# Graph blocks on one core: host-made transposes, norms applied on ScalarE, and a new step order

## The reference, cut to what matters

```python
# block 0
deg = jnp.sum(adj, axis=-1, keepdims=True)
agg = jnp.einsum('bij,bjf->bif', adj, x) / jnp.maximum(deg, EPS)
out = relu(einsum('bnf,of->bno', concatenate([x, agg], axis=2), W))
# block 1: three layers, relu after the first two
adj @ (x @ W) + b
# block 2: 8 heads of 64
attn = softmax(q k^T * scale, masked) * LA + LG * adj + LD * exp(-adj)
out = (attn @ v) @ W_out + b_out
# block 3
w = softmax(sum((q k^T * inv_scale) * adj, axis=-1), axis=nodes)
out = w * v
# after each block
(x - mean) / sqrt(var + 1e-5)
```

## Time and profile before

| | |
|---|---|
| median of 3 runs | 1419.85 us |
| the profiled execution | 1420.36 us |
| its span, first to last instruction | 1418.3 us |
| TensorE busy, share, matmuls | 1373.4 us, 97%, 11152 |
| VectorE busy, share | 1232.1 us, 87% |
| ScalarE busy, share | 921.4 us, 65% |
| GpSimd busy, share | 131.3 us, 9% |
| HBM read, written | 21.90 MB, 8.39 MB |
| mean granted clock of TensorE | 0.987 of 2.4 GHz |

### The profile page before, as it was taken

One profiled execution on the slowest core, in us unless ns is written; L12 is line 12 of the kernel. 1 busy time (PEld: TensorE's weight loads), 2 busy tenths in 40 slices (PEclk: granted clock), 3 DMA queues, 4 the chain that ended last, 5 costly groups with the idle time before them and its releaser, 6 DMA issues.

```text
span 1418.3 us, 30311 instructions
## 1 busy us (share of the span) xinstructions
PE 1373.4 (97%) x11152; PEld 1218.3 (86%) x11152; DVE 1232.1 (87%) x3821; ACT 921.4 (65%) x2445; POOL 131.3 (9%) x265
## 2 busy tenths in 40 slices
PE   4799999999999999999999999999999999999995
PEld 4788889888889888889888889888888888889884
DVE  4688889889889889889889889889889989889985
ACT  4466766666776666776666776666676666676662
POOL 0000001101001101001101001100001100001100
PEclk8899999999999999999999999999999999999997
DMA  4000000000000000000000000000000000000000
GB/s 146 17 17 17 24 24 2 24 24 25 24 24 4 22 24 25 24 25 9 17 24 24 24 25 11 15 25 24 24 25 20 6 25 24 24 25 9 1 9 22
DMA packets 34050, 32.22 MB, mean 23 GB/s; under 512 B 6896, under 2 KB 33392, under 8 KB 33904
## 3 DMA queue, kind: packets, MB, share of 16 engines
q1 hardware_dynamic: 33904, 30.30, 6.8%
HBM read 21.90 MB, written 8.39 MB: 21 GB/s over the span
## 4 chain that ended last, share of the span: by engine, by line
PE 96%; DVE 1%; ACT 1%; DMA 1%; issue 0%; POOL 0%; SPq 0%; POOLq 0%; DVEq 0%; ACTq 0%
PE psum L911 62%; PE psum L925 14%; PE psum L1143 9%; PE psum L1118 8%; PE psum L1192 1%; PE psum L1195 1%; DMA w_raw<-in_L_gnn_W 1%; PE psum L1205 0%; PE psum L1213 0%; DVE bn L561 0%; ACT wqkv_h L309 0%; POOL rstd L294 0%; DVE x L598 0%; ACT work L444 0%; DVE w_l L545 0%
## 5 line engine op out<-in xcount | busy, mean ns | idle before, releaser
L444 ACT ACTIVATE work<-work,shift 128x256 f32<-128x256 f32 x512 | 254.1, 500 | 16.5 <-DVE shift L738 16.5
L757 DVE SCALAR_TENSOR_TENSOR work<-work,rsum,extra 128x256 f32<-128x256 f32 x512 | 223.2, 478 | 1.4 <-DVE rsum L749 0.2
L738 DVE CUSTOM_DVE_ANT_0 work<-psum,minus_big 128x256 f32<-128x256 f32 x512 | 190.1, 419 | 2.2 <-PE psum L1118 1.6
L309 ACT ACTIVATE work<-psum 128x512 f32<-128x512 f32 x256 | 147.3, 591 | 10.0 <-PE psum L925 9.8
L291 POOL TENSOR_TENSOR mv<-mv,eps 128x2 f32<-128x2 f32 x128 | 34.4, 269 | 1272.8 <-DVE mv L582 1272.8
L911 PE MATMUL psum<-x2T_h,wqkv_h 128*128 128x256 f32 x512 | 149.2, 291 | 1.2 <-DVE x2T_l L545 1.2
L911 PE MATMUL psum<-x2T_l,wqkv_h 128*128 128x256 f32 x512 | 143.3, 280 | 0.0
L911 PE MATMUL psum<-x2T_h,wqkv_l 128*128 128x256 f32 x512 | 143.0, 279 | 0.0
L925 PE MATMUL psum<-ident,work 128*128 128x128 f32 x1024 | 139.8, 274 | 0.1
L1143 PE MATMUL psum<-work,v_sb 128*64 128x256 f32 x1024 | 131.9, 389 | 0.9 <-ACT work L309 0.7
L309 ACT ACTIVATE qkT_h<-psum 128x512 fp32r<-128x512 f32 x128 | 76.6, 599 | 85.7 <-PE psum L911 85.7
(11 more groups left out here) (138 smaller groups left out, 3858.1 us busy)
## 6 DMA issues: line engine op xcount, KB each, us to landing
x_sb<-in_x SPq DMA_DIRECT2D x32, 256.0 KB, 2.8
adj_sb<-in_adj SPq DMA_DIRECT2D x32, 256.0 KB, 3.0
out<-y_sb SPq DMA_DIRECT2D x32, 256.0 KB, 2.1
work<-in_L_gnn_W_qkv SPq DMA_DIRECT2D x1, 1536.0 KB, 9.0
mask_row<-in_nodemask SPq DMA_DIRECT2D x32, 32.0 KB, 3.4
w_raw<-in_L_gnn_W SPq DMA_DIRECT2D x3, 256.0 KB, 6.9
w_raw<-in_L_gnn_W SPq DMA_DIRECT2D x1, 512.0 KB, 8.2
wout_raw<-in_L_gnn_W_out SPq DMA_DIRECT2D x1, 512.0 KB, 9.8
```

The lines of the kernel that those rows point to most:

```text
L309: return nc.scalar.activation(dst, src, ACT.Copy, scale=scale)
L444: last = nc.scalar.activation(prob[:, p % 2, i, h], prob[:, p % 2, i, h], ACT.Exp, bias=shift[:, p % 2, h, i:i + 1], scale=-1.0, accum_out ...
L738: last = V_.tensor_tensor_reduce(out=prob[:, p % 2, i, h], in0=bank(SCORES[p] + h)[:, i * N:(i + 1) * N], in1=minus_big[:, g % 2, i], scal ...
L757: last = V_.scalar_tensor_tensor(out=prob[:, p % 2, i, h], in0=prob[:, p % 2, i, h], scalar=rsum[:, p % 2, h, i:i + 1], in1=extra[:, g % 2 ...
```

## The change

**Inputs.** The host hands in four more arrays: x and adj with their last two axes exchanged (`xT`, `adjT`), the weights of block 0 transposed in halves (`L0_gnn_WT`), and the two weights of block 3 joined and transposed (`L3_gnn_WT`); the three original weights of these blocks are no longer inputs. x and adj themselves are still loaded. `x_transpose`, `adj_transpose` and `weight_transposes` are gone from TensorE; the high and low parts are now made from SBUF instead of PSUM.

**Semaphores.** `dma_graph` is replaced by five pairs (`dma_x`, `dma_adj`, `dma_mask_row`, `dma_xT`, `dma_adjT`), and each step waits for its own input. At the start the transposed x and the weights of block 0 are issued first; the weights of block 3 come last and are split after those of block 2's output.

**Norms.** `norm_apply` moves from VectorE to ScalarE, as one ACTIVATE (Identity) per half with a scale and a bias per partition. GpSimd makes the bias, -mean x root, with two more operations per norm.

**Order and banks.** All four slot lists and the table of banks are new. Cut to its core:

```diff
-        XT = 6
-        ADJT = 2
-        SUP0 = 1
-        SELF = 7
-        AGG = 2
+        SUP0 = 7
+        SELF = 2
+        AGG = 6
...
+            def load_x(g):
+                fetch(xT_sb, xT_d, g, dma_xT)
+
+            def load_rest(g):
+                fetch(adjT_sb, adjT_d, g, dma_adjT)
+                fetch(adj_sb, adj_d, g, dma_adj)
+                fetch(x_sb, x_d, g, dma_x)
...
                 nc.gpsimd.tensor_tensor(mv[:, k, :, 1], mv[:, k, :, 1], eps[:, :], ALU.add) \
                     .then_inc(pool_var[k], 1)
+                nc.gpsimd.tensor_tensor(minus_mean[:, k], mv[:, k, :, 0], minus_one[:, :], ALU.mult) \
+                    .then_inc(pool_mean[k], 1)
                 pool.wait_ge(pool_var[k], once(g))
                 nc.gpsimd.tensor_tensor(rstd[:, k], mv[:, k, :, 1], minus_half[:, :], ALU.pow) \
+                    .then_inc(pool_pow[k], 1)
+                pool.wait_ge(pool_pow[k], once(g))
+                pool.wait_ge(pool_mean[k], once(g))
+                nc.gpsimd.tensor_tensor(minus_mean[:, k], minus_mean[:, k], rstd[:, k], ALU.mult) \
                     .then_inc(pool_rstd[k], 1)
...
-                act.wait_ge(pe_xT, once(g))
-                copy(fT[0][:, :, :], halves(bank(XT))).then_inc(act_xT, 1)
+                act.wait_ge(dma_xT[g % 2], loaded(g))
+                copy(fT[0][:, :, :], xT_sb[:, g % 2]).then_inc(act_xT, 1)
...
+            def norm_apply(k, g):
...
+                act.wait_ge(pool_rstd[k], once(g))
...
+                if k == 2:
+                    reuse(act, dve_x4_pre, once(g - 1))
...
+                for t in range(NT):
+                    last = nc.scalar.activation(dst[:, t], src[:, t], ACT.Identity, bias=minus_mean[:, k, t:t + 1],
+                                                scale=rstd[:, k, t:t + 1])
+                last.then_inc(act_y if k == 3 else act_x[k], 1)
...
-                pe.wait_ge(dve_x[0], once(g))
-                reuse(pe, act_probT, nth2(g - 1, 0, 1))
+                pe.wait_ge(act_x[0], once(g))
                 transpose_tiles(bank(X1T), x1).then_inc(pe_x1T, 1)
```

TensorE's new list, in which graph s - 1 is in block 1, s - 2 in attention and s - 3 in the tail:

```diff
             def slot(s):
+                qk(s - 2, 1)
+                tail_project(s - 3, HI)
+                tail_project(s - 3, LO)
+                scores(s - 2, 0)
+                scores(s - 2, 1)
+                tail_adj_k(s - 3)
+                values(s - 2, HI)
+                aggregate(s - 1, HI)
+                aggregate(s - 1, LO)
+                qk(s - 2, 2)
+                values(s - 2, LO)
+                qk(s - 2, 3)
+                probs_t(s - 2, 0, 0)
+                scores(s - 2, 2)
+                x1_transpose(s - 1)
+                probs_t(s - 2, 0, 1)
+                probs_t(s - 2, 1, 0)
+                support(0, s - 1, HI)
+                support(0, s - 1, LO)
+                probs_t(s - 2, 1, 1)
+                scores(s - 2, 3)
+                hidden(0, s - 1, HI)
+                hidden(0, s - 1, LO)
+                attend(s - 2, 0)
+                attend(s - 2, 1)
+                support(1, s - 1, HI)
+                support(1, s - 1, LO)
+                gate_row(s - 3)
+                probs_t(s - 2, 2, 0)
+                probs_t(s - 2, 2, 1)
+                hidden(1, s - 1, HI)
+                hidden(1, s - 1, LO)
+                probs_t(s - 2, 3, 0)
+                probs_t(s - 2, 3, 1)
+                attend(s - 2, 2)
+                support(2, s - 1, HI)
+                support(2, s - 1, LO)
+                attend(s - 2, 3)
+                gcn_out(s - 1, HI)
+                gcn_out(s - 1, LO)
+                support0(s, HI)
+                project_out(s - 2, HI)
+                project_out(s - 2, LO)
+                support0(s, LO)
+                x2_transpose(s - 1)
+                gate_column(s - 3)
+                self_product(s)
+                qk(s - 1, 0)
+                x3_transpose(s - 2)
```

More of the change, by code:

```diff
@@ new lines, in slot @@
+                exps(s - 6, 3, 1)
+                sup_hi(1, s - 5)
+                out_hi(s - 6, 0)
+                probs_t(s - 6, 2, 0)
+                probs_t(s - 6, 2, 1)
+                out_hi(s - 6, 1)
+                hidden(1, s - 5)
+                hidden_hi(1, s - 5)
+                probs_t(s - 6, 3, 0)
+                probs_t(s - 6, 3, 1)
+                sup_hi(2, s - 5)
+                x_hi(s - 4)
+                out_hi(s - 6, 2)
+                mask_bias(s - 4)
+                out_hi(s - 6, 3)
@@ new lines, in slot @@
+                gate_exps(s - 7)
+                adj_exp(s - 4)
+                norm_apply(1, s - 5)
+                x2_hi(s - 5)
+                gate_column(s - 7)
+                degrees(s - 4)
+                norm_apply(2, s - 6)
+                qk_hi(s - 5, 0)
+                sup0_hi(s - 4)
+                x3_hi(s - 6)
+                qk_hi(s - 5, 1)
+                tail_qkv(s - 6)
+                adj_hi(s - 4)
+                self_copy(s - 4)
+                norm_apply(3, s - 7)
@@ new lines, in slot @@
+                exps(s - 5, 0, 0)
+                exps(s - 5, 0, 1)
+                exps(s - 5, 1, 0)
+                qk_hi(s - 5, 2)
+                exps(s - 5, 1, 1)
+                values(s - 5)
+                norm_apply(0, s - 4)
+                qk_hi(s - 5, 3)
+                probs_t(s - 5, 0, 0)
+                x1_hi(s - 4)
+                probs_t(s - 5, 0, 1)
+                probs_t(s - 5, 1, 0)
+                sup_hi(0, s - 4)
+                probs_t(s - 5, 1, 1)
+                exps(s - 5, 2, 0)
@@ L533, in _ @@
+                exps(s - 5, 2, 1)
+                hidden(0, s - 4)
+                hidden_hi(0, s - 4)
             masks()
@@ new lines, in slot @@
+                scores(s - 4, 0, 0)
+                scores(s - 4, 0, 1)
+                adj_lo(s - 3)
+                scores(s - 4, 1, 0)
+                scores(s - 4, 1, 1)
+                tail_gate(s - 5)
+                aggregate(s - 3)
+                relu_residual(s - 3)
+                recip_sums(s - 4, 0)
+                norm_stats(0, s - 3)
+                norm_mean(0, s - 3)
+                probs(s - 4, 0, 0)
+                qk_lo(s - 4, 2)
+                recip_sums(s - 4, 1)
@@ new lines, in slot @@
+                probs(s - 4, 0, 1)
+                probs(s - 4, 1, 0)
+                probs(s - 4, 1, 1)
+                x1_lo(s - 3)
+                qk_lo(s - 4, 3)
+                scores(s - 4, 2, 0)
+                scores(s - 4, 2, 1)
+                sup_lo(0, s - 3)
+                scores(s - 4, 3, 0)
+                scores(s - 4, 3, 1)
+                recip_sums(s - 4, 2)
+                probs(s - 4, 2, 0)
+                probs(s - 4, 2, 1)
+                hidden_lo(0, s - 3)
@@ new lines, in slot @@
+                recip_sums(s - 4, 3)
+                probs(s - 4, 3, 0)
+                sup_lo(1, s - 3)
+                probs(s - 4, 3, 1)
+                out_lo(s - 4, 0)
+                gate_maximum(s - 5)
+                x1_bias(s - 3)
+                hidden_lo(1, s - 3)
+                adj_sum(s - 3)
+                sup_lo(2, s - 3)
+                out_lo(s - 4, 1)
+                x_lo(s - 2)
+                out_lo(s - 4, 2)
+                out_lo(s - 4, 3)
+                gcn_out(s - 3)
```

413 lines of the change are left out of this document (130 added, 283 removed).

## The result

| | before | after |
|---|---|---|
| median of 4 runs each | 1421.38 us | 1473.8 us |
| lowest, highest | 1418.3, 1423.34 | 1470.3, 1476.66 |
| the profiled execution, its span | 1420.36, 1418.3 | 1476.49, 1474.7 |

The changed kernel is slower: ratio 1.037, 95% interval 1.0333 to 1.0406. The prediction was 1412, and its range ended at 1437.

What follows compares the result with a forecast made beforehand. TensorE, without idle time at 42.36 us a slot, bounds the kernel. Savings of 1.24 less waits of 1.08 give 42.18; 1420.4 - 5.6 (31 slots) - 2.2 (ends) = 1412.6, said as 1412, range 1379 to 1437.

Steps and rivals of the forecast that it cites:

- The floor of TensorE in the new order: TensorE's starts per slot: 42.36 less 0.89 for transposes and 0.35 for fewer switches, 41.1 us.
- ScalarE's application: Norm application on ScalarE: 0.59 us one, pair ending at 1.08, against VectorE's pair at 0.74; +0.34.
- x3's wait: TensorE's wait at x3's transposes, from the end of project_out: 0.2 to 0.5, taken as 0.4 us.
- Three waits, 1.08 us a slot: TensorE waits before the x1, x2 and x3 transposes, summing to 1.08 us against 1.24 saved.
- GpSimd's part: Each norm, GpSimd's first start to the application: 1.00 us plus 0.37 for two added operations, about 1.37.
- x2: x2's transposes, from the end of gcn_out: cover 4.28 us against a chain of 4.69, wait 0.41.
- x1: x1's transposes, from the end of aggregate: cover 5.17 us against a chain of 5.44, wait 0.27.
- the parts outside the 31 slots: First and last graph: start -4.0, four lone norms +2.8, transposes and switches gone -1.0; sum -2.2 us.
- the bounds (0.27 to 0.8): Range for GpSimd's two added operations per norm, around 0.37 us.
- Rival 2: Norm chain outweighs savings at the three transposes through GpSimd's slow rows: slot 43.4, about 1450 us; chance 0.25.
- 0.89 us of transposes: TensorE, per graph: four adj transposes removed, 0.36 us, and four of x, 0.53 us.
- rival 3: VectorE's work sets the slot, so TensorE's saving is not given back: 42.36 stays, 1418 us; chance 0.06.

Runs made afterwards that it cites:

- quiet: Changed kernel with two VectorE steps, adj_extra and x2_bias, moved ahead of gcn_out and nothing removed; 1455.0 us.
- swap: Changed kernel with the two waits of VectorE's aggregate step back in the old order, TensorE's product first; 1462.42 us.
- one_pool: Changed kernel with the epsilon add and the mean's negation moved from GpSimd to VectorE, norms still applied on ScalarE; 1434.68 us.
- inputs_only: Kernel before with the host's transposed inputs alone, order and norms as before; 1411.77 us.
- norm_dve: Changed kernel with norms applied on VectorE again and two GpSimd operations a norm, transposed inputs and new order kept; 1448.55 us.
- quiet_dve: norm_dve with adj_extra and x2_bias ahead of gcn_out, aggregate's waits in the old order, and norm 1's application behind gate_probs; 1425.71 us.
- act_norm: Kernel before with norms applied on ScalarE and four GpSimd operations a norm, inputs and TensorE and VectorE order as before; 1502.28 us.
- ports: Separate kernel timing GpSimd's small operations alone and beside each kind of VectorE operation; root 0.67 us alone, 1.20 beside tensor_tensor with two SBUF inputs.

## Why the prediction was wrong

**What was right.** The floor of TensorE in the new order, 41.1 predicted, 41.3 measured. ScalarE's application: 0.593 us one, 1.09 the pair, predicted 0.59 and 1.08 (the row below; mean ns of one is the second number after the bar). The Trainium skill's 93 ns for each pointer (ScalarE: Activation LUTs, section What ACT_TABLE_LOAD costs) agrees for the second one too: 0.409, 0.500, 0.593. x3's wait, 0.4 predicted, 0.40. And the place of the loss: three waits at the transposes.

```profile
L400 ACT ACTIVATE x<-x_pre,minus_mean,rstd 128x256 f32<-128x256 f32 x192 | 104.8, 593 | 93.2 <-POOL minus_mean L316 69.9
```

**The step that failed: "Three waits, 1.08 us a slot".** They measured 2.81. One term of the chains was mis-sized, GpSimd's part (1.37 us), and one was missing, VectorE's late start ahead of norm 0. The sizes below are read from the trace of after:
- x2: predicted 0.41, measured 1.25. GpSimd's part took 2.15 us instead of 1.37, 0.78 more, and 0.41 + 0.78 = 1.19. Its cause is `adj_extra` and `x2_bias`, which the new order puts right behind the norm's statistics on VectorE. quiet moves them and GpSimd's part falls to 1.34; the wait fell only by 0.24 there, because the moved steps delay VectorE elsewhere.
- x1 and pair 0's probabilities: predicted 0.27, measured 0.72 + 0.44 = 1.16. GpSimd 1.83 instead of 1.37, 0.46 more; the late start on VectorE 0.44 more; 0.27 + 0.90 = 1.17. swap shows the second (0.42 a slot; the late start had delayed the probabilities too, which stand behind the statistics on VectorE). For the first there is one_pool (0.11 of x1's wait left), but the late start fell by 0.37 in it as well, so it does not part the two.
- x3: right.
The 1.73 us beyond the forecast make 54 us over 31 slots, the floor's 0.2 another 6, and the parts outside the 31 slots, predicted at -2.2, came out at +1.8 (56.4 - 54.6), 4 more: 1412.6 + 54 + 6 + 4 = 1477, against 1476.49 profiled. Those last 4 us go with this execution's clock more than with the kernel: two other executions of after are 5 to 6 us shorter. The start gave more than I said (4.7 us still at x1's first transposes), and the stretch behind it, at a granted clock of 0.53, took it back. In swap's execution, at 0.90 there, the parts outside come to 98.2 us (1452.9 - 31 x 43.70), against 105.1 in before and 107.0 in after.

**What I misread.** I had the cause in hand: the sum at 0.20 us and 1.00 from it to the application in one place, 0.34 and a root of 0.81 in another. I took that for a spread of GpSimd's own and put it into the bounds (0.27 to 0.8). It was mostly a question of order: which VectorE instruction runs beside it. Had I laid VectorE's new list beside each norm, x2's place would have shown two that read two SBUF tensors. Rival 2 had the mechanism and the sign, "GpSimd's slow rows for all four operations", and ended at 1450 because it priced GpSimd's part at 0.57 over the forecast's (measured: 0.78 at x2, 0.46 at x1) and because it did not know the late start of 0.44.

**The saved time.** That 0.89 us of transposes would come off was taken for granted in the forecast, and rival 3 had 6 in 100. In the old order inputs_only shows 0.16 of it; of the rest, another 0.16 went to GpSimd's slower root. In the new order it did come off, in the floor, and was then spent in the waits.

**Where the parts stand.** Inputs alone -10 us, norms alone +82 (34 of them by my placement), all three +52. norm_dve against inputs_only has the same inputs and nearly the same norms and differs by the order: +37. So the new order, with the applications where I put them on VectorE, costs the old norms 37 us, and 14 with the repairs (quiet_dve); what it saves the new ones cannot be told from these runs, because act_norm's placement is not that of the change.

**Open.** Why the step on the aggregate starts 0.48 us behind its product in after, 0.04 in swap with the two waits exchanged, and 0.11 in quiet and one_pool with the waits of after. Why a root beside the same VectorE step took 1.42 us in some slots of norm_dve and 0.81 in others. Why a root beside scalar_tensor_tensor took 0.68 in ports but 0.92 in one_pool's x1 norm:

```profile
619.51 0.92 POOL L307 TENSOR_TENSOR rstd<-mv,minus_half 128x2 f32<-128x2 f32 x1 [7.65 <-DVE mv L622]
```

## What to carry to other kernels

Price a small GpSimd operation by what VectorE runs beside it, not by its mean: one row at 0.2 and another at 0.34 are two neighbours, and the order decides which one you get. That holds for a change of memory too: a VectorE step that reads an operand from SBUF instead of PSUM is another neighbour. Work taken off a busy engine comes back only if no other engine used that time to get ready; look at what each removed step had been covering, and at what each moved step releases, buffers included. Then move one step and look again: a wait taken away here twice turned up one step on, and a time that comes out as expected (quiet) can be the sum of other parts.
